# Attention on Trainium2: the product with values with one head per column tile instead of one key block per column tile

## What is computed

```python
q = hidden_state @ Wq + bq
k = encoder_hidden_state @ Wk + bk
v = encoder_hidden_state @ Wv + bv
scores = jnp.einsum('bkgld,bksd->bkgls', q, k) * scale + mask
attn = jax.nn.softmax(scores, axis=-1)
out = jnp.einsum('bkgls,bksd->bkgld', attn, v)
out = out.transpose(0, 3, 1, 2, 4).reshape(b, l, H) @ Wo + bo
x = out + hidden_state
return (x - mean(x)) * rsqrt(var(x) + EPS) * gamma + beta
```

## Time and profile before

| | |
|---|---|
| median of the runs | 1751.18 us (1751.04 to 1751.32, 2 runs) |
| span of the profiled execution | 1749.3 us |
| PE busy | 1602.6 us (92%), 14048 matmuls and 14048 weight loads |
| DVE busy | 1448.7 us (83%) |
| ACT busy | 1385.7 us (79%) |
| POOL busy | 935.7 us (53%) |

### The profile page before, as it was taken

How to read it: one execution, slowest core, us unless ns; L and a number is a source line. 1 busy time by engine, 2 the same in 40 slices (tenths; PEclk the granted TensorE clock), 3 DMA queues, 4 the chain that set the end, 5 groups by cost and what they waited for, 6 DMA issues and landing times. The chain is left out here.

```text
span 1749.3 us, 38438 instructions
## 1 busy us (share of the span) xinstructions
PE 1602.6 (92%) x14048; PEld 1110.0 (63%) x14048; DVE 1448.7 (83%) x2773; ACT 1385.7 (79%) x3186; POOL 935.7 (53%) x731
## 2 busy tenths in 40 slices
PE   3898879999899989999899998999989999999986
PEld 2665556576566765676576775667666676667654
DVE  4489878789788996889888898789988899788886
ACT  3578868769888787978889789787888878887794
POOL 5426433526754458534675448662585545856382
PEclk8999999999999999999999999999999999999998
DMA  9669987646885578664796567965678646875331
GB/s 178 186 148 227 241 232 199 182 135 168 250 257 144 138 187 286 188 154 122 209 288 185 130 175 192 287 178 127 174 238 252 158 133 170 292 208 150 84 114 67
DMA packets 357292, 325.02 MB, mean 186 GB/s; under 512 B 145776, under 2 KB 248176, under 8 KB 357104
## 3 DMA queue, kind: packets, MB, share of 16 engines
q1 hardware_dynamic: 357104, 322.56, 67.5%
HBM read 244.85 MB, written 83.89 MB: 188 GB/s over the span
## 5 line engine op out<-in xcount | busy, mean ns | idle before, releaser
L1941 PE MATMUL bank<-ring_hi,w_sb 128*128 128x512 f32 x2368 | 785.5, 399 | 32.1 <-issue 19.2
L1725 ACT ACTIVATE probs<-probs,shift 128x512 f32<-128x512 f32 x1024 | 726.9, 713 | 92.1 <-DVE shift L1826 91.0
L1839 DVE STREAM_TRANSPOSE turned_p<-probs 128x2048 f32<-128x2048 f32 x256 | 585.7, 2297 | 154.3 <-PE bank L2021 149.3
L1826 DVE CUSTOM_DVE_ANT_0 probs<-bank,mask_l 128x512 f32<-128x512 f32 x1024 | 643.1, 680 | 56.3 <-PE bank L2001 37.2
L1626 POOL TENSOR_TENSOR w_sb<-w_raw,w_sb 128x512 fp32r<-128x512 f32 x320 | 412.1, 1297 | 413.8 <-ACT w_sb L1682 413.7
L1941 PEld LDWEIGHTS bank<-ring_hi,w_sb 128*128 128x128 f32 x2368 | 444.4, 189 | 149.9 <-issue 42.6
L1941 PE MATMUL bank<-ring_lo,w_sb 128*128 128x512 f32 x1184 | 467.9, 395 | 0.0
L2001 PE MATMUL bank<-k_stack,q_stack 96*128 96x512 f32 x1024 | 358.9, 414 | 12.7 <-DVE shift L1826 10.0
L2021 PE MATMUL bank<-turned_p,v_all 32*32 32x512 f32 x8192 | 307.9, 642 | 65.8 <-DVE turned_p L1839 48.6
L1638 POOL TENSOR_TENSOR ring_lo<-x_t,ring_hi 128x512 fp32r<-128x512 f32 x168 | 214.7, 1291 | 144.9 <-ACT ring_hi L1694 144.4
L2001 PEld LDWEIGHTS bank<-k_stack,q_stack 96*128 96x128 f32 x1024 | 186.1, 189 | 143.3 <-issue 62.9
(11 more groups left out here) (75 smaller groups left out, 933.2 us busy)
## 6 DMA issues: line engine op xcount, KB each, us to landing
w_raw<-w_d SPq DMA_DIRECT2D x144, 256.0 KB, 3.7
q_stack<-q_hi_d SPq DMA_DIRECT2D x128, 256.0 KB, 4.3
w_raw<-in_L_xattn_Wo_dram SPq DMA_DIRECT2D x128, 256.0 KB, 3.0
q_hi_d<-part_hi SPq DMA_DIRECT2D x64, 256.0 KB, 3.9
q_lo_d<-part SPq DMA_DIRECT2D x64, 256.0 KB, 5.0
q_stack<-q_lo_d SPq DMA_DIRECT2D x64, 256.0 KB, 3.9
v_all<-v_d SPq DMA_DIRECT2D x256, 64.0 KB, 2.2
out_dram<-y_sb SPq DMA_DIRECT2D x32, 512.0 KB, 3.0
```

Source lines behind the costliest of these rows:

```text
L1725: nc.scalar.activation(probs[:, st % 2, h, :], probs[:, st % 2, h, :], ACT.Exp, scale=-1.0, bias=shift[:, g % 2, i:i + 1], accum_out=sums[ ...
L1826: nc.vector.tensor_tensor_reduce(out=probs[:, st % 2, h, :], in0=S_ps[h][:, :], in1=mask_l[:, st, :], scale=-1.0, scalar=HIGHEST, op0=ALU. ...
L1839: nc.vector.transpose(turned_p[:, :, :, st, :].rearrange("p j h c -> p h j c"), probs[:, st % 2, :, :].rearrange("p h (j c) -> p h j c", c ...
L1941: mm = nc.tensor.matmul(C[c][:, :], w_sb[:, n_w, (1, 0, 0)[third], d % 4, :], (hi, lo, hi)[third], start=(n == 0), stop=(n == 23))
```

## The change

The product with values gives each column tile a head instead of a key block. For each key block j, head h and row group r there is one product of 32x32 values with the 128 columns of that head, which adds on in bank 4 + r, partitions 32h to 32h+31, columns 0 to 127, over all 16 key blocks. Nothing is left to be added across partitions, so "sel", "pick", "pv_out" and pv_sb go. "norm" reads the four banks directly (128 columns of each) and is ordered 4.2 us behind the place of "pv". The row sums come first: "recip" and "spread" are ordered just ahead of the group's fourth turn, "rbc" 1.5 us and "rbc_out" 1.0 us ahead of "pv", in bank 7, and "pv" waits for rbc_out since it writes that bank. o_sb has two buffers. Waits that were on pv_out or rbc_out are on normed. The places of all other steps stay.

```diff
+NORM_BEHIND = 4.2
...
+                put(at["turn"][g][3] - 0.02, "recip", g)
+                put(at["turn"][g][3] - 0.01, "spread", g)
                 for n in range(4):
                     put(at["turn"][g][n], "turn", g, n)
-                    put(at["pv_out"][g][n], "pv_out", g, n)
...
-                put(at["pv"][g], "pv", g, PV_PARTS - 1)
-                for what in ("recip", "spread", "v_load", "sel", "rbc", "rbc_out", "norm"):
-                    put(at[what][g], what, g)
+                put(at["pv"][g] - 1.5, "rbc", g)
+                put(at["pv"][g] - 1.0, "rbc_out", g)
+                put(at["pv"][g], "pv", g)
+                put(at["pv"][g] + NORM_BEHIND, "norm", g)
+                put(at["v_load"][g], "v_load", g)
...
-        R_ps, Y_ps, O_ps = bank[6], bank[6], bank[7]
+        Y_ps, R_ps = bank[6], bank[7]
...
-                elif kind == "pv_out" and not (group(t, e[1]) == NG * NB - 1 and e[2] >= 2):
...
-                    nc.scalar.activation(pv_sb[:, r, :], PV_ps[r][:, :], ACT.Copy).then_inc(pv_out, 1)
...
-                    dve.wait_ge(sel_done, G + 1)
+                    dve.wait_ge(pv_done, G + 1)
                     dve.wait_ge(rbc_out, G + 1)
...
-                    nc.vector.tensor_tensor(o_sb[:, :], O_ps[:, :], r_all[:, :], ALU.mult).then_inc(normed, 1)
+                    rows = "p (a r c) -> p r a c"
+                    nc.vector.tensor_tensor(o_sb[:, G % 2, :].rearrange(rows, a=LT, r=4),
+                                            O_ps[:, :, 0:P].rearrange("p r (a c) -> p r a c", a=LT),
+                                            r_all[:, :].rearrange(rows, a=LT, r=4), ALU.mult).then_inc(normed, 1)
...
                     if x in WINDOW and group(t, WINDOW[x]) > 0:
-                        pe.wait_ge(pv_out, 4 * (group(t, WINDOW[x]) - 1) + c + 1)
+                        pe.wait_ge(normed, group(t, WINDOW[x]))
...
-                    for jj in range(4 * n // PV_PARTS, 4 * (n + 1) // PV_PARTS):
-                        for c in range(4):
-                            for r in range(4):
-                                j = 4 * jj + c
-                                mm = nc.tensor.matmul(PV_ps[r][32 * c:32 * (c + 1), :],
-                                                      v_all[32 * r:32 * (r + 1), g % 2, HD * j:HD * (j + 1)],
-                                                      turned_p[32 * r:32 * (r + 1), j, :, :, :]
-                                                      .rearrange("p h a c -> p (h a c)"),
-                                                      start=(jj == 0), stop=(jj == 3))
...
+                    pe.wait_ge(rbc_out, G + 1)
+                    wait(pe, normed, G)
+                    for j in range(NJ):
+                        for h, r in itertools.product(range(GH), range(4)):
+                            mm = nc.tensor.matmul(O_ps[32 * h:32 * (h + 1), r, 0:P],
+                                                  v_all[32 * r:32 * (r + 1), g % 2, HD * j:HD * (j + 1)],
+                                                  turned_p[32 * r:32 * (r + 1), j, h, :, :].rearrange("p a c -> p (a c)"),
+                                                  start=(j == 0), stop=(j == NJ - 1))
+                    mm.then_inc(pv_done, 1)
...
-                elif kind == "sel":
...
-                    for h in range(GH):
-                        mm = nc.tensor.matmul(O_ps[HD * h:HD * (h + 1), :]
-                                              .rearrange("p (a r c) -> p r a c", a=LT, r=4), pick[:, :],
-                                              pv_sb[:, :, P * h:P * (h + 1)].rearrange("p r (a c) -> p r a c", c=32),
-                                              start=True, stop=True)
-                    mm.then_inc(sel_done, 1)
```

More of the change, by code:

```diff
@@ L1693, in _ @@
                     used_up(act, *x)
-                    nc.scalar.activation(chunk_at(*x)[0], o_sb[:, :] if what == "E" else x_t[:, TURN[x] % 2, :],
+                    nc.scalar.activation(chunk_at(*x)[0], o_sb[:, d % 2, :] if what == "E" else x_t[:, TURN[x] % 2, :],
                                          ACT.Copy).then_inc(hi_done, 1)
@@ L1742, in _ @@
                     wait(act, normed, G)
-                    nc.scalar.activation(r_all[:, :], sums_bank(t, e[1])[:, :], ACT.Copy).then_inc(rbc_out, 1)
+                    nc.scalar.activation(r_all[:, :], R_ps[:, :], ACT.Copy).then_inc(rbc_out, 1)
                 elif kind == "root":
@@ L1794, in _ @@
                       .then_inc(x_turned, 1)
-                elif kind == "pv_out" and group(t, e[1]) == NG * NB - 1 and e[2] >= 2:
-                    r = e[2]
-                    if r == 2:
-                        dve.wait_ge(pv_done, NG * NB)
-                        dve.wait_ge(sel_done, NG * NB - 1)
-                    nc.vector.tensor_copy(pv_sb[:, r, :], PV_ps[r][:, :]).then_inc(pv_out_v, 1)
                 elif kind == "x_lo" and (t == -1 and e[1] == "X" or e[1:] == ["E", 7]):
@@ L2003, in _ @@
                 elif kind == "pv":
-                    g, n = e[1:]
+                    g = e[1]
                     G = group(t, g)
-                    if n == 0:
-                        pe.wait_ge(turned, 4 * (G + 1))
-                        pe.wait_ge(v_in[g % 2], 64 * (4 * t + g // 2 + 1))
-                        for c in range(2):
-                            pe.wait_ge(c_free[c], tiles_until(t, g, c))
-                        if t == NB - 1 and g >= 5:
-                            pe.wait_ge(row_kept, 4 * (g - 4))
-                        wait(pe, normed, G)
-                        if g in Y_TURN.values():
-                            wait(pe, y_added, y_before(t, g))
@@ new lines, in _ @@
+                    pe.wait_ge(v_in[g % 2], 64 * (4 * t + g // 2 + 1))
+                    for c in range(2):
+                        pe.wait_ge(c_free[c], tiles_until(t, g, c))
+                    if t == NB - 1 and g >= 5:
+                        pe.wait_ge(row_kept, 4 * (g - 4))
+                    if g in Y_TURN.values():
+                        wait(pe, y_added, y_before(t, g))
+                    pe.wait_ge(rbc_out, G + 1)
[6 more added lines that the diff above has]
+                                                  start=(j == 0), stop=(j == NJ - 1))
@@ L2055, in _ @@
                     pe.wait_ge(c_free[m % 2], TILE[t, what, m])
-                    pe.wait_ge(rbc_out, group(t, Y_TURN[m]))
+                    pe.wait_ge(normed, group(t, Y_TURN[m]))
                     if m > 0:
```

82 lines of the change are left out of this document (24 added, 58 removed).

## The result

The changed kernel takes 2440.9 us (median of 2 runs, 2434.6 to 2447.3) where the kernel before takes 1751.2: a ratio of 1.394, with a 95% interval of 1.386 to 1.403, or +690 us. The profiled execution has a span of 2432.8 us. I had forecast 2350 with a range up to 2620: the direction, the mechanism and the size of the main term were right; several smaller terms had the wrong size, and one rested on a wrong premise.

A forecast was written before the change was run, and what follows sets the result against it. PE was taken as the bound, busy 1602.6 of 1749.3 us. Per group 9.3 + 2.0 - 1.4 + 0.3 = 10.2 us, x 64 = 653, less 50: 1751 + 600 = 2350 us, range 1970 to 2620.

The forecast's parts named there:

- The arrival of code decides, not its issue: Product with values on PE: issuing alone would take 4.9 us, but waiting for code blocks makes it 14.1 against 4.81.
- rival A: Code keeps up with PE, several blocks under way: product takes 4.9 us, kernel gets faster, 1687 us; chance 0.12.
- Rival D: A fixed price per instruction, 37.6 ns per matmul with its load: product takes 19.2 us, kernel 2600 us; chance 0.06.
- Two blocks of 256 instructions: PE's sequencer holds two code blocks of about 256 instructions and asks for the next on entering the second.
- +9.3 for the product: Product with values, per group: three waits for code of 5.0, 3.8 and 3.8 us, then 1.5; 14.1 us against 4.81.
- T: Time from PE's request for a code block to getting it: DMA queue wait, packet, 1.35 us; at least 2.3 us.
- rival B: Code-bound but mild: T = 3.4 us throughout and the clock stays up, product 11.7 us, kernel 2070 us; chance 0.20.
- C's 5.3: Code-bound and harsh rival: T = 5.3 us throughout, product 18.7 us, kernel 2740 us; chance 0.08.
- The clock, +2.0 us a group: After each product the clock is at 1.2 GHz, so what follows runs at half speed for some 4 us.
- "sel", -1.4 us a group: Selection matmuls on PE go: 1.1 us of matmuls and 0.36 us before their loads saved per group.
- The row sums, +0.3 us a group: Waits for POOL's spread and rbc_out ahead of the product on PE, beside the fourth turn; bounds 0 and 1.5.
- -50 us for turn waits that vanish: While PE stands, DVE and ACT catch up, so most of PE's 48.6 us of waits for turns goes.

The follow-up runs named there:

- experiment 2: Kernel before with each 512-column product with values issued as four of 128 columns, in the same banks: 2428.3 us, ratio 1.385.
- experiment 4: Changed kernel with only 32 instead of 128 columns streamed in 240 of a group's 256 products: 2431.2 us in one execution.
- experiment 5: Kernel before with 1024 extra small products at PE's start, the first 512 with SP's loads held back, the rest beside loads: 1798.1 us in one execution.
- experiment 9: Kernel before with each group's four 512-column selection products replaced by one of 32 columns, leaving out the sum over partial products: 1743.6 us, ratio 0.994.
- experiment 6: Kernel before with only recip, spread, rbc and rbc_out moved ahead, the product waiting for rbc_out: 1808.8 us, ratio 1.031.
- experiment 10: Changed kernel with rbc and rbc_out put behind the product again, which no longer waits for rbc_out: 2474.3 us, ratio 1.414.
- experiment 1: Changed kernel with the product again as 64 products of 512 columns a group, the addition over column tiles left out: 1812.3 us, ratio 1.035.

## Why the prediction was right, and where it was not

- **The arrival of code decides, not its issue: right.** The instructions do come fast when they are there, 128 matmuls in 1.89 us, 14.8 ns each, and then PE stands; experiments 2 and 4 show that it is their number and not the columns. But 128 of them were reckoned at 9.0 ns a load, 1.2 us, from 31 loads in the kernel before; a whole block takes 1.89. By that rate, an estimate, issuing alone would take 512 x 14.8 ns = 7.6 us and not 4.9, so that even rival A's product would have been longer than the one before. Rival A (1687 us) is out: no product runs through. Rival D, a price per instruction, is out as well, since bursts and stops alternate. The Trainium skill ("TensorE: Matmul & The Clock Gate", "Wait — 56ns, not 53.3ns?") has a floor of 25 ns between starts. It doesn't hold across these tiles, at 14.8 ns.
- **Two blocks of 256 instructions: right.** The bursts have exactly 128 matmuls and 128 loads, 3.3 stops a product and one where the product has 512 instructions. By the Trainium skill ("Runtime: NRT & Kernel Launch", "Instruction fetch mechanics") there are two lines of 256, and the trace agrees. The same section has the fetch as mostly hidden. That is so in the kernel before, where 256 instructions of the product are followed by 512-column work and its waits for "issue" are 3.7 us, and not in this one, where they are 349 us.
- **The term "+9.3 for the product": right, in size and nearly in its parts.** Forecast 14.1 us, measured 14.5 on the average. In the timeline 46 of the 64 products have four bursts, the middle two of 128 matmuls. In these the next burst begins on the average 5.0 us after the start, then 4.1 and 3.7 us on, and the last one lasts 1.4 us; the forecast had 5.0, 3.8, 3.8 and 1.5. Part of that is luck: the model had only the queue ahead of the packet, so that T would fall towards 2.3 us on idle queues. There at least 1.0 us passes first, and T stays at 3.45 or more (experiment 5, and the timeline above). The 3.8 us came out, as I read it, because that latency was contained in the durations seen before. Of 125 intervals between the later bursts of the kernel after, 107 are 3.4 to 4.0 us and 7 over 5: rival B's T = 3.4 is the least that occurs, and C's 5.3 is rare.
- **The clock, +2.0 us a group: too much.** Projections and scores, the same instructions, took (811.4 - 785.5) + (486.0 - 467.9 for ring_lo) + (393.8 - 358.9) = 79 us more, 1.2 a group. The step that failed is "the new product works about 1.2 us of every 3.8 and should do the same": 128 matmuls take 1.89 us and not 1.2, and the clock is at 0.50 (1.2 GHz) behind 31 of the 64 products and not behind all. In the example above it is back at 1.00 (2.4 GHz) in two stretches with stops of 1.60 us. In experiment 4, where PE works less between the stops, it is at 0.50 behind all 64, and the mean falls from 0.875 to 0.79.
- **"sel", -1.4 us a group (90 us): failed.** Experiment 9 gives 10 us in all. What failed is the premise "what PE is spared counts nearly in full": PE was busy for 92%, but with less work it waited more (19 us, half of it for shift) and had a lower granted clock. In the other direction the premise held: the added 9.7 us a group did count in full.
- **The row sums, +0.3 us a group: too little for the short product, covered with the long one.** Alone they cost 55 us, 0.9 a group (experiment 6), inside the bounds 0 to 1.5. In the kernel after, a place behind the product gives none of it back (experiment 10): there their waits are those of the fourth turn under another name, the cover that the prediction named.
- **-50 us for turn waits that vanish: no gain.** They did vanish (48.6 to 0.9), but r_wide, r_all, part and shift took 42.7, 15.2, 23.3 and 28.5 us, against 6.1 and 10.0 before for the last two. The prediction didn't ask what PE would wait for in their place, beyond the 0.3 us for the row sums.

As a sum: the instructions alone, by experiment 1, cost 629 us where the forecast had 64 x 11.3 - 50 = 673; the other edits were to give 70 and cost 60. -44 and +130 are 86 of the 91 us between 2350 and 2441, the rest is rounding. So that the total came out within 4% is in part luck: the instructions came out 44 us cheaper than forecast, which hides a third of what the other edits missed. (By experiment 2 the instructions cost 676 us and the other edits the remaining 14; which of them one undoes first matters.) In experiment 1 the 60 us can be put down as 55 for the row sums, -10 for sel and some 15 left. That rest is a difference, which assumes that the parts add up; the wait for shift, 61.8 us against 10.0 before, points to "norm", for which DVE now stands behind the product, but no run isolates it.

Only experiment 9 was faster than the kernel before, by 0.6%, and it leaves out work. Accumulating in place with one head per column tile asks for products of 128 columns; whether the turned probabilities can be laid out so that it needs fewer, wider ones was not tried and is open.

## What to carry to other kernels

Count a stretch's instructions as well as its columns: an fp32 product on a 32x32 tile was four of them here (two loads, two matmuls), and PE had two blocks of 256 at hand. Beyond those every further 256 took 3.5 to 4 us on idle DMA queues and 6 to 7 beside heavy loads, whatever they do, so products should be long enough that 256 instructions last that long. And take the gain of sparing an engine at 92% not at its face value: 53 us less work on PE here gave 10, since the next wait and the clock took the rest.

## What the runs showed that I had not expected

- A code packet has a latency of its own with nothing queued: 1.0 to 1.4 us from the start of the burst to its own, 1.1 to 1.2 for 16.4 KB, 1.2 to 1.6 to the first instruction, 3.45 to 4.0 us in all where it was looked at with idle queues, at a granted clock of 1.00 and of 0.50 alike.
- With 53 us of TensorE work removed, the mean granted clock was 0.964 in place of 0.974, and the scores took 368.5 us in place of 358.9.
- The right place of the row sums depends on the length of what follows: putting them ahead costs 55 us with products of 4.8 us, and putting them behind costs 34 with products of 14.5.
